# A kernel of deformable attention, token attention and a mixture of experts: where keys and values are projected and sampled

## The reference

```python
q = conv1x1(x, wq)                                  # x is group-normed
off = ...                                           # depthwise 5x5 conv of q, norm, gelu, w_off: 3 x 4x4
offset = tanh(off[:, 0:2]) / 4
dm = jax.nn.sigmoid(off[:, 2])[:, None]             # a gate for each sample
pos = offset + ref_points(Hk, Wk)[None]
xs = grid_sample(x.reshape(B * G, gc, H, W), pos[..., ::-1])
xs = (xs * dm).reshape(B, C, 1, n)
k = conv1x1(xs, wk).reshape(B * nH, dh, n)
v = conv1x1(xs, wv).reshape(B * nH, dh, n)
attn = jnp.einsum('bcm,bcn->bmn', qf, k) * scale
attn = jax.nn.softmax(attn + bias, axis=2)          # bias: a table sampled at query minus pos
out = jnp.einsum('bmn,bcn->bcm', attn, v)
```

## Time and profile before

| what | us |
| --- | --- |
| median of 3 runs | 60.29 |
| lowest, highest | 60.23, 61.31 |
| the profiled execution | 60.18 |
| its span, first to last instruction | 58.4 |
| TensorE busy in it | 51.2 |
| VectorE, ScalarE, GpSimd busy | 37.0, 29.7, 18.4 |

### The profile page before, as it was taken

One profiled execution on the slowest core, in us unless ns is written; L12 is line 12 of the kernel. 1 busy time (PEld: TensorE's weight loads), 2 busy tenths in 40 slices (PEclk: granted clock), 3 DMA queues, 4 the chain that ended last, 5 costly groups with the idle time before them and its releaser, 6 DMA issues.

```text
span 58.4 us, 1532 instructions
## 1 busy us (share of the span) xinstructions
PE 51.2 (88%) x622; PEld 42.7 (73%) x622; DVE 37.0 (63%) x95; ACT 29.7 (51%) x65; POOL 18.4 (31%) x41
## 2 busy tenths in 40 slices
PE   3996996999699699999999998979999899979920
PEld 3995894986388579889897986636689498868800
DVE  3379399965659989449993055839267764785320
ACT  0802042787999804104844776197973739701020
...
PEclk9999999999999999999999999999999999999999
...
DMA packets 3927, 2.04 MB, mean 35 GB/s; under 512 B 2640, under 2 KB 3792, under 8 KB 3920
## 3 DMA queue, kind: packets, MB, share of 16 engines
...
HBM read 1.67 MB, written 0.26 MB: 33 GB/s over the span
## 4 chain that ended last, share of the span: by engine, by line
PE 60%; DVE 12%; POOL 8%; ACT 6%; DMA 4%; issue 4%; DVEq 0%; ACTq 0%
PE ps L680 5%; PE ps L761 4%; DMA x_sb<-x_rows 4%; PE ps L805 4%; PE ps L754 4%; PE ps L826 3%; PE ps L884 3%; PE ps L867 3%; PE ps L783 3%; DVE taps L1069 3%; POOL w_smp L486 2%; PE ps L889 2%; ACT e_tok L621 2%; PE ps L1001 2%; DVE off L1071 2%
## 5 line engine op out<-in xcount | busy, mean ns | idle before, releaser
L680 PE MATMUL ps<-zeros 128*128 128x128 bf16 x164 | 12.7, 235 | 1.0 <-DVE zeros L1046 1.0
L680 PEld LDWEIGHTS ps<-zeros 128*128 128x128 bf16 x164 | 11.4, 107 | 1.6 <-DVE zeros L1046 1.0
L511 ACT ACT_TABLE_LOAD x4 | 5.1, 1283 | 1.7 <-PEq L1283 1.6
L621 ACT ACTIVATE e_tok<-ps,cst 128x512 f32<-128x512 f32 (+1 forms) x6 | 4.5, 827 | 1.5 <-PE ps L867 1.5
L1100 DVE COPY_PREDICATED ps<-over,ps 128x608 f32<-128x608 uint32 (+1 forms) x4 | 3.1, 777 | 0.8 <-PE ps L733 0.7
L733 PE MATMUL ps<-rpe_blk,minus_hat_rel 128*32 128x168 f32 x64 | 2.8, 316 | 0.5 <-DVE minus_hat_rel L1096 0.5
L571 ACT ACTIVATE kv<-ps,cst 128x256 f32<-128x256 f32 x4 | 1.7, 471 | 2.8 <-PE ps L754 2.8
L733 PEld LDWEIGHTS ps<-rpe_blk,minus_hat_rel 128*32 128x32 f32 x64 | 2.0, 142 | 1.3 <-issue 0.9
L439 POOL TENSOR_TENSOR wblk<-wts,cst 128x256 f32<-128x256 f32 x3 | 2.1, 687 | 2.3 <-DMA wts<-weights 2.3
L884 PE MATMUL ps<-e_tok,t 128*32 128x128 f32 (+1 forms) x48 | 2.8, 310 | 0.0
L1147 DVE TENSOR_REDUCE ln_ss<-ln_sq 128x8 f32<-128x264 f32 x2 | 0.9, 428 | 3.0 <-ACT ln_sq L601 3.0
...
## 6 DMA issues: line engine op xcount, KB each, us to landing
...
wts<-weights SPq DMA_DIRECT2D x1, 192.5 KB, 4.4
...
```

Source lines behind the costliest of these rows:

```text
L511: nc.scalar.add_instruction(mybir.InstLoadActFuncSet(name=nc.get_next_instruction_name(), act_func_set_id=functions, ins=[], outs=[]))
L621: return nc.scalar.activation(dst, scores, ACT.Exp, bias=const("bound"))
L680: mm(bank(n_bank, P), zeros[:, :], zeros[:, :], start=True, stop=True)
```

## The change

Keys and values are projected from all tokens of the normed image before the sampling: for each token half two matmuls with a stationary of tokens and 256 moving columns (project, after.py's L712) give tokens by (group, image, channel), called k_tok and v_tok. The samples are then taken from these: an output block of 32 channels (two images) by 32 samples (the same two images) is one matmul of 128 tokens, and 32 of them, over 2 input groups, 2 output groups, 4 pairs of images and 2 token halves, add up in one bank that a matmul on zeros has cleared. The gate is multiplied into the hat of x (hat_gate, VectorE), and so into w_smp; its factor 0.5 sits in the key weights and in the value copy. The mask matmul, xn_tok, xs and the gate product go. A pair's block also holds samples of the one image with channels of the other; the copies for each head leave them out, by four copies of 128 elements instead of two of 256. Of the logits, those of the first query half are all added before the second half's key matmul. Values are sampled after the logits.

```diff
...
@@ -41,3 +41,3 @@
 BUSY = {
-    "xn_ready": 45, "off_ready": 22, "off_blk_ready": 28, "w_smp_ready": 20, "xs_ready": 8,
+    "xn_ready": 45, "off_ready": 5, "off_blk_ready": 14, "w_smp_ready": 2,
     "d_prob_ready": 0, "prob_copied": 3, "t1_ready": 2, "t1_second": 3, "g_low_ready": 8,
...
@@ -447,2 +450,5 @@
             pool.wait_ge(weights_loaded[1], 16)
+            link(nc.gpsimd.tensor_scalar(wk_s[:, :, :], wkvo[:, 0], 0.5 * QK_SCALE, None, ALU.mult))
+            for g in range(G):
+                blocks(wblk[:, 1, g], wk_s[:, g].rearrange("p (g o) -> p g o", g=G), G, GC).then_inc(wk_ready, 1)
             pool.wait_ge(const_loaded[2], 16)
...
@@ -454,5 +460,3 @@
                 ALU.mult).then_inc(rpe_blk_ready, 1)
-            link(nc.gpsimd.tensor_scalar(wk_s[:, :, :], wkvo[:, 0], QK_SCALE, None, ALU.mult))
             for g in range(G):
-                blocks(wblk[:, 1, g], wk_s[:, g].rearrange("p (g o) -> p g o", g=G), G, GC).then_inc(wkvo_ready, 1)
                 blocks(wblk[:, 2, g], wkvo[:, 1, g].rearrange("p (g o) -> p g o", g=G), G, GC).then_inc(wkvo_ready, 1)
...
@@ -484,4 +488,5 @@
             pool.wait_ge(hat_smp_ready, 1)
+            pool.wait_ge(hat_gate_ready, 1)
             for h in range(NHALF):
-                nc.gpsimd.tensor_tensor(w_smp[:, h], hat_smp[:, h], hat_smp[:, 2], ALU.mult).then_inc(w_smp_ready, 1)
+                nc.gpsimd.tensor_tensor(w_smp[:, h], hat_smp[:, h], hat_gate[:, :], ALU.mult).then_inc(w_smp_ready, 1)
             link(nc.gpsimd.tensor_tensor(tap_both[:, :, :], tap_next[:, :, :], tap_prev[:, :, :], ALU.add))
...
@@ -525,5 +530,6 @@
 
-            act.wait_ge(xn_turned, 1)
-            nc.scalar.activation(xn_tok[:, :, :, :], xnt_ps, ACT.Copy, scale=0.5).then_inc(xn_tok_copied, 1)
             copy_q(0)
+            copy_q(1)
+            act.wait_ge(ktok_done, 1)
+            nc.scalar.activation(k_tok[:, 0], ktok_ps[0], ACT.Copy).then_inc(ktok_copied, 1)
             act.wait_ge(centered, 1)
...
@@ -553,11 +558,12 @@
 
-            for k in range(3):
-                distance(a_smp, k, 0 if k < NHALF else 1, "at_pixel").then_inc(a_smp_ready, 1)
-
-            act.wait_ge(a_smp_ready, 3)
-            nc.scalar.activation(hat_smp[:, :, :], a_smp[:, :, :], ACT.Relu, bias=1.0, scale=-1.0).then_inc(
-                hat_smp_ready, 1)
-
             act.wait_ge(off_done, 4)
             nc.scalar.activation(half_tanh[:, :], off_ps[2], ACT.Tanh, scale=0.5).then_inc(half_tanh_ready, 1)
+            distance(a_smp, 2, 1, "at_pixel").then_inc(a_smp_ready, 1)
+            act.wait_ge(a_smp_ready, 1)
+            nc.scalar.activation(hat_smp[:, 2], a_smp[:, 2], ACT.Relu, bias=1.0, scale=-1.0).then_inc(hat_x_ready, 1)
+            for k in range(NHALF):
+                distance(a_smp, k, 0, "at_pixel").then_inc(a_smp_ready, 1)
+            act.wait_ge(a_smp_ready, 3)
+            nc.scalar.activation(hat_smp[:, 0:NHALF], a_smp[:, 0:NHALF], ACT.Relu, bias=1.0, scale=-1.0).then_inc(
+                hat_smp_ready, 1)
             load_table(LN_EXP_SET)
...
@@ -567,16 +573,25 @@
 
-            def copy_heads(w, ready):
+            def keep_tokens(h):
 
-                for hh in range(HG):
-                    nc.scalar.activation(kv[:, w, :, :, hh], kv_ps[w].rearrange("p g (t j) -> p g t j", t=NT), ACT.Copy,
-                                         scale=const("head")[:, hh:hh + 1]).then_inc(ready, 1)
+                act.wait_ge(vtok_done, h + 1)
+                nc.scalar.activation(v_tok[:, h], vtok_ps[h], ACT.Copy, scale=0.5).then_inc(vtok_copied, 1)
 
+            def copy_head(w, hh, ready):
+
+                pairs_ps = kv_ps.rearrange("p g (t q s n) -> p (g t) q s n", t=NT, s=2, n=N)
+                pairs_sb = kv[:, w].rearrange("p g t k (q s n) -> p (g t) k q s n", s=2, n=N)
+                for side in range(2):
+                    nc.scalar.activation(pairs_sb[:, :, hh, :, side], pairs_ps[:, :, :, side], ACT.Copy,
+                                         scale=const("head")[:, 2 * hh + side:2 * hh + side + 1]).then_inc(ready, 1)
+
+            keep_tokens(0)
             act.wait_ge(k_done, 1)
-            copy_heads(0, k_ready)
-            act.wait_ge(d_sub_ready, 1)
-            nc.scalar.activation(d_exp[:, 0], d_sub[:, 0], ACT.Exp).then_inc(d_exp_ready, 1)
-            act.wait_ge(v_done, 1)
-            copy_heads(1, v_ready)
-            act.wait_ge(d_sub_ready, 2)
-            nc.scalar.activation(d_exp[:, 1], d_sub[:, 1], ACT.Exp).then_inc(d_exp_ready, 1)
+            for hh in range(HG):
+                copy_head(0, hh, k_ready)
+            keep_tokens(1)
+            for h in range(NHALF):
+                act.wait_ge(d_sub_ready, h + 1)
+                nc.scalar.activation(d_exp[:, h], d_sub[:, h], ACT.Exp).then_inc(d_exp_ready, 1)
+                act.wait_ge(v_done, 1)
+                copy_head(1, h, v_ready)
             act.wait_ge(vo_done, 1)
...
@@ -693,9 +708,14 @@
 
-            pe.wait_ge(const_loaded[1], 16)
-            for h in range(NHALF):
-                for g in range(G):
-                    last = nc.tensor.transpose(xnt_ps[:, h, g], xn[:, g, h * P:(h + 1) * P], ident)
-            last.then_inc(xn_turned, 1)
+            def project(outputs, w, h, done):
+
+                for gi in range(G):
+                    last = mm(outputs[h][:, gi].rearrange("p g o -> p (g o)"), xn[:, gi, h * P:(h + 1) * P],
+                              wblk[:, w, gi].rearrange("p g b o -> p (g b o)"), start=True, stop=True)
+                last.then_inc(done, 1)
+
+            pe.wait_ge(wk_ready, G)
+            project(ktok_ps, 1, 0, ktok_done)
             keep_busy("off_ready", 7)
 
+            pe.wait_ge(const_loaded[1], 16)
             pe.wait_ge(off_ready, G)
...
@@ -704,14 +724,10 @@
             mm(var_ps, const("avg"), off_sq[:, :], start=True, stop=True).then_inc(var_done, 1)
-            pe.wait_ge(const_loaded[3], 16)
-            mm(off_ps[2].rearrange("p (g b n) -> p g b n", g=G, b=B), const("shut"),
-               same_b.unsqueeze(1).unsqueeze(3).to_broadcast([P, G, B, N]), start=True, stop=False)
-            keep_busy("off_blk_ready", 5)
-
+            project(ktok_ps, 1, 1, ktok_done)
+            keep_busy("off_blk_ready", 6)
 
             pe.wait_ge(off_blk_ready, 1)
-            pe.wait_ge(xn_tok_copied, 1)
             cols = off_blk[:, :, :, :].rearrange("p g b n -> p (g b n)")
 
-            def offset(j, start=True):
-                return mm(off_ps[j], weight("w_off")[:, j:j + 1].to_broadcast([P, P]), cols, start=start, stop=True)
+            def offset(j):
+                return mm(off_ps[j], weight("w_off")[:, j:j + 1].to_broadcast([P, P]), cols, start=True, stop=True)
 
...
@@ -737,22 +753,31 @@
                 last.then_inc(rows_done, 1)
+            pe.wait_ge(half_tanh_ready, 1)
+            pe.wait_ge(txh_ready, 1)
+            pe.wait_ge(wkvo_ready, G)
+            project(vtok_ps, 2, 0, vtok_done)
+            pe.wait_ge(ktok_copied, NHALF)
             keep_busy("w_smp_ready", 5)
 
-            pe.wait_ge(half_tanh_ready, 1)
-            pe.wait_ge(w_smp_ready, 2)
-            for g in range(G):
-                for h in range(NHALF):
-                    last = mm(xs_ps[:, g], xn_tok[:, h, g], w_smp[:, h, g * P:(g + 1) * P],
-                              start=(h == 0), stop=(h == NHALF - 1))
-            last.then_inc(sampled, 1)
-            keep_busy("xs_ready", 6)
-            pe.wait_ge(xs_ready, 1)
-            pe.wait_ge(wkvo_ready, 4)
-            def project(w):
+            def clear_samples():
 
-                for g in range(G):
-                    for gi in range(G):
-                        last = mm(kv_ps[w][:, g], wblk[:, 1 + w, gi, g].rearrange("p b o -> p (b o)"), xs[:, gi],
-                                  start=(gi == 0), stop=(gi == G - 1))
+                mm(kv_ps, zeros[:, :], zeros[:, :].unsqueeze(1).to_broadcast([P, G, P]), start=True, stop=True)
+
+            def sample(tokens, h):
+
+                for gi in range(G):
+                    for g in range(G):
+                        for j in range(4):
+                            rows = slice(32 * j, 32 * j + 32)
+                            last = mm(kv_ps[rows, g, rows], tokens[:, h, gi, g, rows],
+                                      w_smp[:, h, P * gi + 32 * j:P * gi + 32 * j + 32],
+                                      start=False, stop=(h == NHALF - 1 and gi == G - 1), skip_group_check=True)
                 return last
 
+            clear_samples()
+            for h in range(NHALF):
+                pe.wait_ge(w_smp_ready, h + 1)
+                last = sample(k_tok, h)
+            last.then_inc(k_done, 1)
+            project(vtok_ps, 2, 1, vtok_done)
+
             def turn_on(part, g, h, start=False):
...
@@ -765,6 +790,10 @@
 
-            project(0).then_inc(k_done, 1)
+            def add_keys(h):
+
+                for g in range(G):
```

(53 more changed lines are left out.)

45 lines of the change are left out of this document (24 added, 21 removed).

## The result

| kernel | median, us | lowest, highest | n | ratio to before, 95% |
| --- | --- | --- | --- | --- |
| before | 61.26 | 60.23, 63.14 | 20 | |
| changed | 60.97 | 60.72, 62.63 | 20 | 1.0057 [1.0031, 1.0084] |

The changed kernel is slower by 0.57%, and "no change" lies outside the interval. The ratio compares only runs that lie within 1.5% of the fastest of their own kernel; more runs of before fall outside that, which is why the ratio stands above 1 although the median over all runs of before is the higher one. The profiled execution took 60.98 us against 60.18, its span (first to last instruction) 59.2 against 58.4.

What follows compares the result with a forecast made beforehand. TensorE was taken to bound the kernel, never waiting from 21.5 to 28.9 us. Terms +0.15, +0.47, -0.94 and +0.88 sum to +0.56 on 60.18, so 60.74, and with 0.11 for the median 60.8 us; range 60.3 to 61.3.

Steps and rivals of the forecast that it cites:

- same: The call of a whole-kernel time within 2% of before, 59.1 to 61.5 us; chance 0.81.
- The four terms: Front +0.15, further delay until w_smp starts +0.47, w_smp to first logits -0.94, from there to output products +0.88 us.
- Front, +0.15: Before the centring matmul: an added key projection behind GpSimd's block weights starts it 0.15 us later, at 9.63.
- w_smp, +0.47 beyond the front: GpSimd's weight products wait for the hats on ScalarE, beginning at 18.90 instead of 18.28: 0.62 later, 0.47 beyond the front.
- Sampling at 8 ns: TensorE's narrow sampling matmuls: 64 records per tensor at 8 ns each, 0.51 us a tensor.
- Rival C: Narrow sampling matmuls do not overlap: 31 ns a record, 2.0 us a tensor, +2.0, 62.2 us; chance 0.07.
- First maximum: VectorE's maximum of the first half's logits at 25.23 instead of 25.55; w_smp to logits' end 6.13, not 7.07, -0.94.
- The copies behind the exponential, +0.88: ScalarE's second exponential stands between value heads' copies; first logits to output products take 4.39 instead of 3.51 us, +0.88.
- Rival B: Value heads come in time, TensorE stays the bound, output products start at 28.2: 59.6 us; chance 0.14.
- D: Weights land at 7.3, delaying the first key projection, 0.8 us more before the centring: 61.6 us; chance 0.13.
- E: TensorE's clock falls, filler going from 78 matmuls to 21 and pauses reaching 1 us: 64 us or more; chance 0.05.

## Why the prediction came out as it did

**The mechanism and the time were right; the step from the sum to the call was not.** The time, 60.97, is 0.2 above 60.8, and the sum of stages +0.53 against +0.56. The step that failed is the sentence "Within 2% means 59.1 to 61.5, about what a measurement of this kernel can tell from no change (its three runs span 1.8%)", and with it 0.81 for "same": a slowdown that had been worked out was put at nothing. The result does lie within those 2%, but it is not "no change". Three runs' spread was taken for the resolution; twenty runs of each kernel gave the ratio to within 0.3% on either side, 1.0057 [1.0031, 1.0084], clear of 1. A sum of +0.56, nearly 1%, should have been called slower. My own terms said so: the forecast's own range, 60.3 to 61.3, lay wholly at or above the 60.29 of before.

**The sum is closer than its terms.** The four terms were off by -0.06, -0.06, +0.11 and -0.02. That these cancel to -0.03 is in part luck.

**Front, +0.15: mis-sized, +0.09, and for another cause.** The weights land at 6.0, not 6.5, so the blocks are ready and the projection starts at 7.75 right behind q; nothing of it reaches the centring. The 0.09 is a second wait directly in front of the matmul, a term that the prediction does not have.

**w_smp, +0.47 beyond the front: +0.41.** The order of ScalarE was read rightly: w_smp waits for hat_smp. The two distances took 0.92 to the next, exactly the forecast's 0.40 and 0.52; what was a little cheaper is half_tanh, 0.27 to the next (16.25 to 16.52) instead of 0.33, and the stretch ahead of it.

**Sampling at 8 ns: right.** 32 records in 0.46, as the earlier trace rows had it; 64 in 0.76 with the modelled end of 0.2 is 9 ns each. The Trainium skill's figure (TensorE: Matmul & The Clock Gate, "Wait — 56ns, not 53.3ns?"), about 25 ns from start to start at the least, is not what this trace shows where four blocks of 32 columns are used in turn. Rival C is out.

**First maximum: 25.50, less 0.28 is 25.22, forecast 25.23.** As a stage it gave -0.83 and not -0.94: w_smp began 0.12 earlier than forecast (19.06 less 0.28 against 18.90), but TensorE's first logits, behind GpSimd's left, only 0.04 (22.44 less 0.28 against 22.2). So most of what the hats were early was not passed on, and the instant agrees better than the terms. Copies of 128 elements took 372 ns on average, forecast 0.36.

**The copies behind the exponential, +0.88: +0.86.** TensorE's idle time is there, released by ScalarE's kv; it is 0.80 and not "about 1", because x_nat's matmuls began later than forecast (27.71 less 0.28 is 27.43, against 27.2). Taking the exponential away from between the copies gave 0.66 back, so the prediction's "which is the copies behind the exponential" holds for three quarters of the term; the other 0.2 is the copies themselves. Rival B needed the value heads in time; even with the copies first they end 0.2 too late for it, and the time is 60.25, not B's 59.6.

**Rivals D and E: no part of the result, but real.** The clock stayed at full after pauses of 0.80 and 1.36, and fell after one of 1.91.

**What stays open.** The executions of before lie 1.8 to 3.0 us above their spans, those of every other kernel 1.8 to 1.9. I do not know why. It raises the times of before, and lowers ratios here by up to 0.3%. By spans after is 0.5 to 0.6 longer than before (59.1 against 58.5 to 58.6), nearer to the stages' sum than 0.57% of the time, 0.35 us, is; and the kernel with the copies first is by spans equal to before within 0.1 (58.5).
